# A fused conv-attention and expert kernel: the last image's row scatters pause in every fourth expert step

## The chip, the cores and the metric

One core of a Trainium2 chip (trn2). The metric is the device time of one execution in microseconds, the median of the runs. The profile is of one further execution; its span is longer than the runs' times.

## What is computed

Four images of 128 channels and 32 x 32 pixels pass through three kinds of attention (compressed, selected blocks, windows), a gated sum and a residual. That part fills the first 560 us and isn't touched. Its result t, 1024 tokens of 128 numbers per image, then goes through a mixture of experts, of which only this matters:

```python
logits = xt @ Wr + br                       # 8 experts
top_p, top_idx = top_k(softmax(logits), 2)  # two experts per token
xn = layernorm(xt)                          # no gain or bias yet
xe = xn * ln_g[e] + ln_b[e]
h = gelu(xe @ W1[e] + b1[e])                # 128 -> 512
y = h @ W2[e] + b2[e]                       # 512 -> 128
out = sum over the two chosen experts of weight * y
result = t + out
```

All is float32.

## The kernel before

Each engine has its own instruction stream, written out by hand, and semaphores between them. Tokens are not computed by every expert. Every token is copied twice, once for each expert that it picked, into an array in HBM, `xs_d`, which is sorted by expert. A row is 130 numbers: the 128 of the normalised token, its weight, and the row number where its result belongs. The copying is done by scatters: an indirect DMA issued by GpSimd (POOL) takes 128 rows from `pay` in SBUF and sends each to its place (`scatter_row`, L758). An image has 1024 tokens and two picks, so sixteen scatters (`2 * NT`, NT = 8). All scatters count up one semaphore, `scattered`.

The rows are then handled in tiles of 128, each of a single expert. The images form two batches (`BATCH`, images 0 and 1, images 2 and 3). Each batch has 39 tiles (`NTILE`), 78 in all (`NALL`); the second batch's first tile is number 39. An expert step k does these things, each by its engine:

- PE: the first matrix product for tile k - 3 (L2091), the transposes of tile k's rows (L2105), the second product for tile k - 5 (L2109).
- ACT: copies the expert's weights for tile k + 2 (L1052), gelu of tile k - 3 (L1067).
- DVE: adds the bias to tile k - 5 (L1574), applies gain and bias to tile k (L1579), multiplies tile k - 5 by the token weights (L1586).
- POOL: scatters the finished tile k - 5 to `z_d` in HBM with an indirect DMA (L780). In the text this is called the store of tile k - 5.
- SP: loads rows of tiles ahead of PE into a ring of 12 slots (`load_rows`, L619 and L620). Load n waits for the store of tile n - 12, which frees the slot. The queue is in order.

There are 83 steps (`NSTEP`). The first four run beside the last image's selected attention. The last image's router runs in steps 10 to 15 (`STEP_TT`, `STEP_RT`, `STEP_RK` = 15), so its picks are known only then. Its sixteen scatters are put into POOL's steps from 16 on, one in each, ahead of the step's store. POOL's queue is in order as well: a scatter goes out behind the store of the step before it.

SP asks for the scatters at one place. Before load 39 it runs `rows_written(1)`, which waits for all pad rows, for all 64 scatters of the four images, and for the second batch's table of tiles. Loads 40 and on are behind it in the queue. Between loads 28 and 36 SP also copies eight blocks of pad rows (`tail_pad`, L605). After load 50 it loads image 0's results back from `z_d` (`load_sums`, L632), which DVE adds up and PE transposes after step 49 (L1671).

Of the kernel before, what the change touches and what calls it, by code (L numbers as in the profile page):

```python
# [82 lines left out]
XROOM, WROOM, YROOM, HROOM = 8, 4, 8, 2  # L83
NSTEP = NALL + Y_LAG

SCATTER_OF = 100
PAD_AT = 28
ROWS_EARLY = 0
STEP_AT = 7
# [193 lines left out]
def build(nc, x, wqkv_c, wqkv_s, wqkv_w, w1k, w1v, w2k, w2v, gate_w1, gate_w2, projs, wr, fw1, fw2, fb1,  # L283
# [3 lines left out]
    with ExitStack() as ctx:  # L287
# [377 lines left out]
        def _(pool):  # L665
# [85 lines left out]
            def scatter_row(b, k, t):  # L751

                if t == 0:
                    pool.wait_ge(pay2_ready if k else pay_ready, b + 1)
                    if k:
                        pool.wait_ge(pay_ready, b + 1)
                    pool.nop(nofuse=True)
                gp.indirect_dma_start(xs_d, bass.IndirectOffsetOnAxis(pos[:, NT * k + t:NT * k + t + 1], 0),  # L758
                                      pay[:, k, t, :], None).then_inc(scattered, 16)
# [47 lines left out]
            for k in range(STEP_RK + 1, NSTEP):  # L807
                if sent < 2 * NT and k % SCATTER_OF != 0:
                    scatter_row(B - 1, sent // NT, sent % NT)
# [1427 lines left out]
```

## Time and profile before

| | us |
|---|---|
| median of 3 runs | 764.18 |
| lowest and highest run | 763.24 to 765.53 |
| span of the profiled execution | 791.0 |
| PE busy | 657.4 (83%) |
| VectorE (DVE) busy | 518.3 (66%) |
| ScalarE (ACT) busy | 427.1 (54%) |
| GpSimd (POOL) busy | 236.0 (30%) |
| scatters of rows by POOL (L758) | 64 of about 1 us |
| stores of tiles by POOL (L780) | 78 of about 1 us |

Times of the rows are microseconds from the start of the profiled span, which is 27 us longer than the median run. PE means the matmul stream, PEld the weight loads beside it, SPq the sequencer of SP. Some programs' names in a row stand for a ring: `xwin` and `wx_room` are both slots of expert weights, `xrow_room` and `qwT` of loaded rows, `xhatT` and `xblk` of finished tiles. Each float32 matmul shows as two records. A releaser in brackets is inferred; "issue" means that the profile shows nothing that the engine waited for.

### The profile page before, as it was taken

How to read it: one execution, taken by the hardware profiler on the slowest of the kernel's cores; microseconds unless marked ns; L12 is line 12 of the kernel's file. 1: busy time of each engine (PE TensorE's matmuls, PEld its weight loads, DVE VectorE, ACT ScalarE, POOL GpSimd, SP SyncE). 2: the span in 40 equal slices, each digit the busy share in tenths (PEclk: the TensorE clock that was granted, in tenths of full speed). 3: DMA queues.
4: the chain of work that ended last, by engine and by line, in shares of the span. 5: the costliest groups of instructions: out<-in, count | busy, mean ns of one | idle time of the engine just before them, and what ended most of it. 6: DMA issues, size and time to landing. Idle time of an engine off the chain costs nothing.

```text
span 791.0 us, 16898 instructions
## 1 busy us (share of the span) xinstructions
PE 657.4 (83%) x5198; PEld 497.5 (63%) x5198; DVE 518.3 (66%) x1757; ACT 427.1 (54%) x1259; POOL 236.0 (30%) x341
## 2 busy tenths in 40 slices
PE   2998999995999997889998687776879868979972
PEld 1684686663577655548664455543778757979971
DVE  4208678858977966887895678779766323554433
ACT  1228725555843563773355375335757545968851
POOL 3100142002024542004353200515243544533540
PEclk9999999997999999799999877857999979999995
DMA  8200000001000010000003700021014222253214
GB/s 304 105 0 28 2 6 1 2 1 54 0 3 5 25 32 27 1 0 5 2 28 94 202 1 1 8 49 52 21 32 132 59 65 72 72 185 89 66 44 163
DMA packets 36331, 40.27 MB, mean 51 GB/s; under 512 B 12164, under 2 KB 27796, under 8 KB 35956
## 3 DMA queue, kind: packets, MB, share of 16 engines
q1 hardware_dynamic: 30388, 27.70, 12.0%
q0 software_dynamic: 4704, 9.40, 3.6%
q10 hardware_dynamic: 1152, 2.10, 0.7%
q8 instruction: 44, 0.72, 0.4%
q14 instruction: 43, 0.35, 0.1%
HBM read 25.87 MB, written 15.17 MB: 52 GB/s over the span
## 4 chain that ended last, share of the span: by engine, by line
DVE 38%; PE 37%; issue 7%; another core or an unknown queue 5%; POOL 3%; DVEq 3%; ACT 3%; DMA 3%; SPq 1%; POOLq 0%; ACTq 0%
DVE nmx L1195 6%; PE ps L1731 6%; PE ps L1671 5%; PE ps L1676 4%; DVE r_P L1205 4%; DVE t_tok L1320 3%; DVE x_tok L1180 3%; PE ps L2091 3%; PE ps L2109 3%; PE ps L1815 3%; DVEq L1573 2%; PE ps L1746 2%; DVE xwin L1579 2%; PE ps L1788 2%
## 5 line engine op out<-in xcount | busy, mean ns | idle before, releaser
L906 ACT ACTIVATE r_P<-ps,nmx 128x225 f32<-128x225 f32 (+1 forms) x192 | 86.1, 470 | 67.3 <-DVE nmx L1195 65.6
L1574 DVE TENSOR_TENSOR hv<-ps,x_sb 128x128 f32<-128x128 f32 x78 | 22.7, 291 | 96.1 <-remote 50.1
L758 POOL DMA_INDIRECT xs_d<-pay,pos x64 | 66.7, 1042 | 61.4 <-DVE r_P L1205 38.6
L1195 DVE TENSOR_REDUCE nmx<-ps 128x4 f32<-128x900 f32 (+1 forms) x64 | 73.3, 1154 | 4.1 <-PE ps L1788 3.4
L780 POOL DMA_INDIRECT z_d<-xhatT,xrow_room x54 | 51.8, 959 | 78.5 <-DVE xhatT L1586 60.9
L1671 PE MATMUL ps<-ident,r_P 128*128 128x128 f32 (+1 forms) x384 | 59.0, 300 | 16.5 <-DVE R L1220 11.9
L1671 PEld LDWEIGHTS ps<-ident,r_P 128*128 128x128 f32 (+1 forms) x384 | 49.3, 162 | 36.0 <-DVE r_P L1205 22.8
L2091 PE MATMUL ps<-xwin,wx_room 128*128 128x128 f32 x416 | 61.2, 291 | 4.8 <-issue 4.2
L682 POOL TENSOR_TENSOR rstd<-vpe,minus_half 128x8 f32<-128x8 f32 x8 | 13.3, 1666 | 167.8 <-DVE vpe L1139 167.8
L2091 PEld LDWEIGHTS ps<-xwin,wx_room 128*128 128x128 f32 x416 | 55.2, 205 | 7.3 <-issue 6.0
L732 POOL TENSOR_TENSOR r_gh<-r_gh,nmw 113x392 f32<-113x392 f32 (+1 forms) x20 | 15.5, 774 | 148.3 <-DVE nmw L1234 148.0
L1746 PE MATMUL ps<-r_vc,w_sb 128*128 128x225 f32 x256 | 58.8, 375 | 0.0
L1746 PEld LDWEIGHTS ps<-r_vc,w_sb 128*128 128x128 f32 x256 | 46.1, 188 | 19.4 <-issue 15.9
L1731 PE MATMUL ps<-r_kc,w_sb 128*128 128x225 f32 x256 | 58.3, 375 | 0.0
L1788 PE MATMUL ps<-kbd,qT 64*128 64x450 f32 x128 | 39.7, 636 | 20.4 <-ACT r_P L906 20.4
L1205 DVE TENSOR_SCALAR r_P<-r_P,rZ 128x225 f32<-128x225 f32 (+1 forms) x192 | 54.1, 345 | 1.7
L1731 PEld LDWEIGHTS ps<-r_kc,w_sb 128*128 128x128 f32 x256 | 46.3, 188 | 6.6 <-issue 0.4
L2109 PE MATMUL ps<-w_sb,r_vc 128*128 x320 | 45.6, 286 | 5.2 <-issue 4.6
L2109 PEld LDWEIGHTS ps<-w_sb,r_vc 128*128 128x128 f32 x320 | 41.3, 200 | 6.4 <-issue 6.2
L1788 PE MATMUL ps<-kbd,qTs 64*128 64x512 f32 x128 | 43.9, 705 | 1.0 <-ACT r_P L906 1.0
L2109 PE MATMUL ps<-w_sb,qT 128*128 x304 | 42.1, 282 | 0.4 <-ACT qT L1067 0.2
L906 ACT ACTIVATION_READ_ACCUMULATOR r_P<-ps,nmx 128x1 f32 x192 | 41.1, 214 | 0.0
(233 smaller groups left out, 1488.4 us busy)
## 6 DMA issues: line engine op xcount, KB each, us to landing
xrow_room<-xs_d SPq DMA_DIRECT2D x54, 65.0 KB
x_sb<-x SPq DMA_DIRECT2D x4, 512.0 KB, 3.6
w_sb<-w1k SPq DMA_DIRECT2D x1, 2048.0 KB, 8.6
w_sb<-w1v SPq DMA_DIRECT2D x1, 2048.0 KB, 13.0
w_sb<-fw SPq DMA_DIRECT2D x1, 2048.0 KB, 9.3
w_sb<-fw SPq DMA_DIRECT2D x4, 512.0 KB, 9.7
r_vw<-z_d SPq DMA_DIRECT2D x8, 256.0 KB
kbdw<-z_d SPq DMA_DIRECT2D x8, 256.0 KB, 5.1
```

The source lines that it names most:

```text
L758: gp.indirect_dma_start(xs_d, bass.IndirectOffsetOnAxis(pos[:, NT * k + t:NT * k + t + 1], 0), pay[:, k, t, :], None).then_inc(scattered, 16)
L780: gp.indirect_dma_start(z_d, bass.IndirectOffsetOnAxis(xrow(n)[:, C + 1:C + 2].bitcast(U32), 0), yrow(n), None).then_inc(y_out[n % XRING], 16)
L906: last = sc.activation(Pb[t % NRING][:, h, 0:m], bank(name)[:, (h % 2) * m:(h % 2) * m + m], ACT.Exp, bias=nmx[:, t % NRING, h:h + 1], acc ...
L1195: ve.tensor_reduce(nmx[:, t % NRING, :].rearrange("p (a h) -> p a h", a=2), v.rearrange("p a (h m) -> p a h m", h=2), AX.X, ALU.max, negat ...
L1205: last = ve.tensor_scalar(v, v, rZ[:, t % NRING, h:h + 1], None, ALU.mult)
L1671: last = tr(bank(name)[0:m, k * j:k * j + k], src, ident[0:k, 0:k])
L1676: mm(bank(name)[:, 0:n], weights, rhs, start=True, stop=True).then_inc(full_sem(name), 1)
L1731: last = mm(bank(f"mk@{h}")[:, NB * a:NB * a + NB], w1k_sb[:, s, C * a:C * a + C], kcT[:, r:r + 2 * NBH - 1:2, c:c + 2 * NBH - 1:2], start ...
L1746: last = mm(bank(f"mv@{h}")[:, NB * a:NB * a + NB], w1v_sb[:, s, C * a:C * a + C], vcT[:, r:r + 2 * NBH - 1:2, c:c + 2 * NBH - 1:2], start ...
L1788: mm(bank(name)[:, 0:2 * m], q[p0:p0 + 64, 128 * t:128 * t + 128], kbd[p0:p0 + 64, :, 0:m], start=True, stop=True).then_inc(full_sem(name), 1)
L2091: last = mm(bank(f"fh{k}")[:, C * c:C * c + C], wx(n)[:, C * c:C * c + C], xe[:, n % 4, :], start=True, stop=True)
L2109: last = mm(bank(name)[:, 0:C], hT(n)[:, 128 * c:128 * c + 128], fw_sb[:, bass.ds(e, 1), W1X + C * c:W1X + C * c + C].rearrange("p a n -> ...
```

## The change

One constant. In the loop that writes POOL's steps, a scatter is put into step k only when k is no multiple of `SCATTER_OF`. With 100 this leaves out nothing between steps 16 and 31. With 4 it leaves out steps 16, 20, 24, 28, 32 and 36, so that the sixteenth scatter is in step 37.

```diff
-SCATTER_OF = 100
+SCATTER_OF = 4
```

The loop that reads it:

```python
sent = 0
for k in range(STEP_RK + 1, NSTEP):
    if sent < 2 * NT and k % SCATTER_OF != 0:
        scatter_row(B - 1, sent // NT, sent % NT)
        sent += 1
    expert_step(k)
```

## Rows read from the trace of the kernel before

**Rows 1.** The page's first line.
```profile
span 791.0 us, 16898 instructions
```

**Rows 2.** Timeline of PE: transposes of steps 39 and 43 (start, duration, line).
```profile
676.18 0.27 PE L2105 MATMUL ps<-ident,xrow_room 128*128 128x128 f32 x1
...
683.76 0.27 PE L2105 MATMUL ps<-ident,xrow_room 128*128 128x128 f32 x1
```

**Rows 3.** Busy time in windows: PE, PEld, DVE, ACT, POOL, clock, DMA share, GB/s.
```profile
620.00:640.00 20.00, 14.10 (x90) 13.52 (x91) 5.33 (x19) 10.75 (x32) 9.87 (x11) 0.85 0.20 58
...
720.00:740.00 20.00, 19.62 (x173) 19.16 (x172) 8.12 (x27) 17.38 (x52) 9.06 (x10) 1.00 0.23 65
```

**Rows 4.** The chain that ended last, 618 to 730 us (start, length, what).
```profile
618.83 4.16 another core or an unknown queue
...
629.70 7.23 another core or an unknown queue
...
642.04 2.59 another core or an unknown queue
...
646.43 4.93 another core or an unknown queue
...
656.53 6.07 another core or an unknown queue
...
727.39 2.21 another core or an unknown queue
```

**Rows 5.** Timeline of PE inside the second of these pieces.
```profile
635.39 0.27 PE L2091 MATMUL ps<-xwin 128*128 128x128 f32 x1 [1.05 <-issue]
```

**Rows 6.** Timeline of POOL, 609 to 689 us.
```profile
609.34 0.96 POOL L758 DMA_INDIRECT xs_d<-pay,pos  x1 [0.30 <-issue]
...
620.99 0.96 POOL L758 DMA_INDIRECT xs_d<-pay,pos  x1 [0.30 <-issue]
...
634.34 0.96 POOL L758 DMA_INDIRECT xs_d<-pay,pos  x1 [0.30 <-issue]
639.44 0.96 POOL L780 DMA_INDIRECT z_d<-xhatT,xrow_room  x1 [4.14 <-DVE xhatT L1586]
...
653.89 0.96 POOL L780 DMA_INDIRECT z_d<-xblk,qwT  x1 [4.47 <-DVE xblk L1586]
...
660.20 0.95 POOL L758 DMA_INDIRECT xs_d<-pay,pos  x1 [0.30 <-issue]
665.11 0.95 POOL L780 DMA_INDIRECT z_d<-xhatT,xrow_room  x1 [3.95 <-DVE xhatT L1586]
...
673.69 0.95 POOL L780 DMA_INDIRECT z_d<-xhatT,xrow_room  x1 [3.19 <-DVE xhatT L1586]
675.16 0.95 POOL L780 DMA_INDIRECT z_d<-xhatT,xrow_room  x1 [0.52 <-issue]
...
688.04 0.95 POOL L780 DMA_INDIRECT z_d<-xhatT,xrow_room  x1 [1.32 <-DVE xhatT L1586]
```

**Rows 7.** The chain again, 688 to 698 us: store of tile 38, SP, the sums.
```profile
688.04 2.40 DMA z_d<-xhatT,xrow_room
...
690.46 0.28 SPq L619
...
691.18 0.34 SPq L620
...
693.01 5.01 DMA r_vw<-z_d
```

**Rows 8.** Timeline of SP: loads 5 to 8, and load 39.
```profile
529.67 3.65 SPq L620 DMA_DIRECT2D xrow_room<-xs_d  x4
...
672.23 0.34 SPq L620 DMA_DIRECT2D xrow_room<-xs_d  x1
```

**Rows 9.** The page's DMA issues: KB each, median us from issue to landing.
```profile
r_P<-xblk SPq DMA_DIRECT2D x32, 8.0 KB, 1.7
...
out<-x_tok ACTq DMA_DIRECT2D x8, 256.0 KB, 2.1
```

## The prediction, made before the change was built

> **What bounds the kernel now.** I read the windows first, then the chain that ended last, then the timelines of POOL, PE and SP. The whole span is 791.0 us [rows 1]; the change touches only the last quarter, where 78 tiles of 128 routed rows go through the experts in 83 steps. Undisturbed, a step costs PE 1.895 us: the row transposes of steps 39 and 43 start at 676.18 and 683.76, four steps in 7.58 us [rows 2]. In 720 to 740 us PE is busy 19.62 of 20 us; in 620 to 640 us, where the scatters in question go out, only 14.10 of 20 [rows 3]. So PE sets the pace except where it is held up, and the question is what holds it up beside the scatters.
>
> The chain gives the gaps. Between 618 and 663 us it has five long pieces put down to "another core or an unknown queue", 4.16, 7.23, 2.59, 4.93 and 6.07 us, 25.0 us in all; later such a piece is about 2.2 us [rows 4]. There is no other core: in these pieces PE's matmuls come one by one, about 1.05 us of idle time before each, with no engine named as releaser [rows 5]. POOL's timeline shows what goes with it. POOL sends two indirect DMAs per step, a scatter of the last image (xs_d<-pay) and the store of a finished tile (z_d<-...), each 0.96 us long and 1.26 us apart when queued. The last before a gap's end stops at 621.95, 635.30 and 661.15 us (start plus length), and the gaps in the chain end at 622.99, 636.93 and 662.60: 1.0, 1.6 and 1.5 us later [rows 4, 6]. I take it as a pattern, not an explanation: PE runs about four steps, then crawls until POOL has emptied its queue. A cycle of four steps with four scatters is 14.45 us (store at 639.44 to store at 653.89), one without any 8.58 us (665.11 to 673.69) [rows 6].
>
> **The change, part by part.** The edit changes the order of POOL's queue alone. Now the sixteen scatters stand in steps 16 to 31. After it, steps 16, 20, 24, 28, 32 and 36 carry none, so they stand in 17-19, 21-23, 25-27, 29-31, 33-35 and 37. Three things follow.
>
> Taken out of the held-up stretch. The scatter of step 16 starts at 609.34 [rows 6], before the first long gap; moving it gains nothing. Those of steps 20, 24 and 28 stand last in POOL's queue while PE is waiting (the ones of 20 and 24 start at 620.99 and 634.34 [rows 6]). Without each, POOL is empty one slot earlier: 1.26 us, or (14.45 - 8.58) / 4 = 1.47 us by the difference of the cycles. Gain 3.8 to 4.4 us, and zero if POOL isn't what PE waits for.
>
> Put into the later stretch. Steps 33 to 35 get three scatters. The cycle that begins with the store at 665.11 takes 8.58 us now. With them POOL has four stores and three scatters: 1.47 us to the second store (as 673.69 to 675.16), six slots of 1.26 us, 1.4 us from the last op's end to the restart (the mean of the three above), and 2.5 us from restart to the next store (636.93 to 639.44) [rows 4, 6], 12.9 us in all. Cost 4.3 us, and zero by the same reason. The two parts cancel to within 0.5 us: I take 0, with -4.4 and +4.3 as ends.
>
> Moved past a wait. This part decides. SP loads the rows of the tiles from xs_d in order. Before row 39, the first of the second batch, it waits for all 64 scatters. Now the last scatter starts at 660.20 [rows 6]; with the 2.40 us that the store of 688.04 takes to land [rows 7] it is in by 662.6, and SP issues load 39 only at 672.23 [rows 8], for PE's use at 676.18 [rows 2]. The wait is free by 9.6 us. After the change the last scatter is that of step 37, queued on POOL behind the store of tile 31, which step 36 makes. What follows is serial:
> - from the transposes of a step to the store that it makes: 683.76 to 688.04, 4.28 us [rows 2, 6]
> - the scatter's slot behind it: 1.26 us
> - from its start to its landing: 2.40 us [rows 7]
> - SP from there to its issue: 690.44 to 691.18, 0.74 us [rows 7]
> - the load of 65 KB to landing has no row; a load of 8 KB takes 1.7 us and a store of 256 KB 2.1 us [rows 9]. I take 1.9, between these ends.
>
> Sum 10.6 us after the transposes of step 36. PE wants the row three steps later, at 3 x 1.895 = 5.7 us, and so waits 4.9 us. By clock times of the profile, with the store of tile 31 at 675.16 [rows 6]: 675.16 + 1.26 + 2.40 + 0.74 + 1.9 = 681.46, against 676.18, is 5.3 us. I take 5.1. It is shorter only where PE is late at step 39 for another reason, and longer by up to 3 us where POOL is behind at step 36.
>
> The Trainium skill ("DMA: Bandwidth & Descriptors", Anatomy of one DMA) states for a DMA issued by GpSimd a fixed 2.0 us plus the bytes over 436e3. An estimate by it for the 65 KB load is 2.15 us; the wait would be 5.3 to 5.6 us. No row here shows this load to landing.
>
> Who waits behind it: SP's loads 40 to 50 queue behind load 39. Unhindered SP issues four in 3.65 us [rows 8], 1.1 us each, faster than PE's 1.9, so only the first is late. Next is the load of image 0's sums, which needs the store of tile 38 and then 5.01 us of DMA [rows 7]; PE waits for it after step 49 already. Tile 38 is made in step 43, behind the new wait, so that stall moves along and doesn't swallow the 5.1 us. Nothing else before the end reads the scatters' semaphore.
>
> **Sum.** 0 + 5.1 = +5.1 us on a profiled span of 791.0. The runs have a median of 764.18, 27 us under the profiled span; the long gaps may be partly an effect of profiling. The new wait is made of DMA latencies and a queue, and I carry it over unchanged: 764.2 + 5.1 = 769.3 us.
>
> **The rivals.**
> (a) Without the profiler the gaps don't exist, and PE never stops among the scatters. POOL then has no rest from 620.99 on. Now, with a scatter in that slot, 23 slots of 1.26 lead to the store of tile 26 at 650.0; with 2.40 + 0.74 + 1.9 its ring slot gives row 38 at 655.0. PE, at 620.99 - 4.28 = 616.7 with step 20, wants it 18 steps later at 650.8, so it waits 4.2 us today. After the change 29 slots lead to the last scatter at 657.5 and to row 39 at 662.6, wanted at 652.7: 9.9 us. The difference is 5.7 us: 769.9. The 27 us speak for it, the coupling of gap and POOL against. It ends where the forecast does, and I count them together.
> The Trainium skill ("Runtime: NRT & Kernel Launch", Instruction fetch mechanics) says that crossing a block of instructions is mostly hidden; by that rule the gaps aren't code loading, or are none without the profiler, which is (a). The trace doesn't settle it: it shows crawling matmuls without a cause [rows 5].
> (b) Faster: the gap is caused by the very scatter that POOL issues while PE is held. The pauses of 20, 24 and 28 fall on those. If each cycle's gap sinks to the short 2.2 us, that is 25.0 - 4 x 2.2 = 16.2 us, less 5.1: 753. Halved, 761. For it: pauses and gaps share a period of four steps. Against: three scatters and four stores stay in each cycle, and the gap's end follows the last op by 1.0 to 1.6 us wherever it stands. It decides from the point where a pause saves over 1.7 us (5.1 / 3).
> (c) No difference: PE reaches step 39 late anyway, since the scatters of 33 to 35 lengthen the gap at step 37, or the pauses save their upper bound and the added ones cost little. 764 to 766.5.
> (d) Much slower: POOL is behind at step 36 by 3 us, and SP, hindered beside POOL's DMAs, stays late for the sums. 773 to 777.
> (e) That the edit does nothing is excluded: by 100 no step from 16 to 31 is divided, by 4 steps 16, 20, 24 and 28 are.
>
> **How the numbers follow.** Forecast with (a): 0.57 (767 to 773). (b): 0.12. (c): 0.20. (d): 0.11. The range 762 to 774 takes in the forecast, (c) and the near edges of (b) and (d), 8 in 10. About 0.3%, 2.3 us, is what a measurement of this kernel can tell from no change. Slower by more: 0.68; within: 0.20; faster: 0.12.
>
> **What would show it.** In the profile of the changed kernel: the last xs_d<-pay stands between the stores of tiles 31 and 32; SP's wait ahead of load 39 is put down to the scatter; the transposes of step 39 come about 7 us after those of step 38, where it is 1.9 now; the gaps at 622, 636 and 651 us end 1.3 us earlier each, and the one at step 37 grows. The forecast is wrong if step 39 comes without a pause, or if the cycles of four steps with scatters shrink to 10 us.

## The result, and the profile after

The change makes the kernel slower: 771.34 us against 764.32 us, medians of four runs each, a ratio of 1.0092 (95% interval 1.0070 to 1.0114), so +7.0 us with an interval of +5.3 to +8.7 us. The forecast was +5.1 us, 769.3.

The spans, though, are 791.0 us [rows 1] and 768.2 us, the wrong way round. One look at a kernel can mislead, and this one did. The kernel before was therefore profiled once more in the first experiment; that span is 763.2 us. All comparisons below use this second look unless they name the first, and the section on the reasons says what it does to the prediction.

The page of the changed kernel, with PE's row of slices and the clock:

```profile
span 768.2 us, 16898 instructions
...
PE 646.4 (84%) x5198; PEld 490.5 (64%) x5198; DVE 518.7 (68%) x1757; ACT 429.7 (56%) x1259; POOL 236.6 (31%) x341
...
PE   2999999995989999598998948778698998799992
...
PEclk9999999997999999799999969856999999999995
```

The windows of the changed kernel, which answer to [rows 3] (length, then busy time of PE, PEld, DVE, ACT and POOL with instruction counts, granted clock as a share of full speed, DMA share, GB/s):

```profile
620.00:640.00 20.00, 18.65 (x162) 18.11 (x161) 8.86 (x28) 16.72 (x48) 15.13 (x16) 1.00 0.38 98
640.00:660.00 20.00, 12.84 (x105) 11.93 (x104) 6.27 (x21) 12.64 (x36) 14.41 (x15) 0.99 0.33 85
...
720.00:740.00 20.00, 20.00 (x182) 20.00 (x181) 9.16 (x32) 17.45 (x53) 9.79 (x11) 1.00 0.26 68
```

In 620 to 640 us PE is busy 18.65 us where the first look at before had 14.10: the long gaps of [rows 4] are gone. The loss is in 640 to 660. Its place shows in PE's timeline of the changed kernel, the row transposes of steps 20, 38, 39, 40 and 41, which answer to [rows 2]:

```profile
612.89 0.27 PE L2105 MATMUL ps<-ident,qwT 128*128 128x128 f32 x1
...
652.88 0.27 PE L2105 MATMUL ps<-ident,xrow_room 128*128 128x128 f32 x1
660.34 0.45 PE L2105 MATMUL ps<-ident,xrow_room 128*128 128x128 f32 x1 [5.40 <-DMA xrow_room<-xs_d]
663.62 0.27 PE L2105 MATMUL ps<-ident,xrow_room 128*128 128x128 f32 x1
665.51 0.27 PE L2105 MATMUL ps<-ident,xrow_room 128*128 128x128 f32 x1
```

and steps 20, 38, 39 and 40 in the second look at the kernel before:

```profile
613.45 0.27 PE L2105 MATMUL ps<-ident,qwT 128*128 128x128 f32 x1
...
655.24 0.30 PE L2105 MATMUL ps<-ident,xrow_room 128*128 128x128 f32 x1 [0.31 <-DMA xrow_room<-xs_d]
657.26 0.27 PE L2105 MATMUL ps<-ident,xrow_room 128*128 128x128 f32 x1
659.16 0.27 PE L2105 MATMUL ps<-ident,xrow_room 128*128 128x128 f32 x1
```

Read as differences, they split the loss. From step 20 to 38 the changed kernel needs 39.99 us, before 41.79: a gain of 1.80. From 38 to 39 it needs 7.46 against 2.02: a loss of 5.44, of which 5.40 stand in the row as idle time ended by the load of the rows. From 39 to 40 it needs 3.28 against 1.90: a loss of 1.38. In all 50.73 against 45.71 us, +5.02. The spans differ by 5.0 as well, because what lies around this stretch cancels: up to step 20 the changed kernel is 0.6 us earlier, and from step 40 to the end it takes 104.6 us against 104.0. The medians differ by 7.0; where the other 2 us come from is told at the end.

The chain that ended last, in the changed kernel, goes through the links that the prediction named (start, length, what); it answers to [rows 7]:

```profile
655.21 2.30 DMA xs_d<-pay,pos
657.51 0.02 SPq L618
...
657.57 0.27 SPq L619
...
658.29 1.91 DMA xrow_room<-xs_d
...
660.34 0.45 PE ps L2105
```

The last scatter starts at 655.21 and lands at 657.51, SP issues load 39 at 658.29, it lands at 660.20, and PE goes on at 660.34. SP's list of waits has 7.6 us for the time that SP stood at the scatters' semaphore:

```profile
SPq L618 <- DMA xs_d<-pay,pos: 7.6, 1, 7.6
```

### The profile page after: what moved, and what is told of

It is laid out like the page before. It is cut to its first block, busy times and chain, and to the rows that moved or that the text cites. A ratio compares the mean times of both kernels' runs of the same rounds, so it can differ in the third digit from the quotient of the medians.

```text
span 768.2 us, 16898 instructions
## 1 busy us (share of the span) xinstructions
PE 646.4 (84%) x5198; PEld 490.5 (64%) x5198; DVE 518.7 (68%) x1757; ACT 429.7 (56%) x1259; POOL 236.6 (31%) x341
## 4 chain that ended last, share of the span: by engine, by line
PE 45%; DVE 35%; issue 6%; DMA 4%; POOL 4%; ACT 3%; SPq 2%; DVEq 1%; POOLq 0%; ACTq 0%
DVE nmx L1195 6%; PE ps L2091 6%; PE ps L1731 6%; PE ps L2109 6%; PE ps L1671 5%; DVE r_P L1205 4%; PE ps L1676 4%; DVE t_tok L1320 4%; PE ps L1815 3%; DVE x_tok L1180 3%; PE ps L1746 2%; PE ps L1845 2%; PE ps L1788 2%; DVE r_gh L1205 2%; ACT r_P L906 2%
## 5 line engine op out<-in xcount | busy, mean ns | idle before, releaser
L1671 PE MATMUL ps<-ident,r_P 128*128 128x128 f32 (+1 forms) x384 | 56.5, 291 | 15.1 <-DVE R L1220 10.7
L1671 PEld LDWEIGHTS ps<-ident,r_P 128*128 128x128 f32 (+1 forms) x384 | 47.0, 156 | 34.1 <-DVE r_P L1205 23.2
L2091 PE MATMUL ps<-xwin,wx_room 128*128 128x128 f32 x416 | 58.1, 285 | 0.0
L2091 PEld LDWEIGHTS ps<-xwin,wx_room 128*128 128x128 f32 x416 | 53.4, 201 | 0.7 <-issue 0.4
L1731 PEld LDWEIGHTS ps<-r_kc,w_sb 128*128 128x128 f32 x256 | 46.4, 188 | 6.6 <-issue 0.4
L2109 PE MATMUL ps<-w_sb,r_vc 128*128 x320 | 43.0, 278 | 0.0
L2109 PEld LDWEIGHTS ps<-w_sb,r_vc 128*128 128x128 f32 x320 | 39.3, 194 | 0.5 <-issue 0.4
```

Source lines behind the costliest of these rows:

```text
L1671: last = tr(bank(name)[0:m, k * j:k * j + k], src, ident[0:k, 0:k])
L1731: last = mm(bank(f"mk@{h}")[:, NB * a:NB * a + NB], w1k_sb[:, s, C * a:C * a + C], kcT[:, r:r + 2 * NBH - 1:2, c:c + 2 * NBH - 1:2], start ...
L2091: last = mm(bank(f"fh{k}")[:, C * c:C * c + C], wx(n)[:, C * c:C * c + C], xe[:, n % 4, :], start=True, stop=True)
L2109: last = mm(bank(name)[:, 0:C], hT(n)[:, 128 * c:128 * c + 128], fw_sb[:, bass.ds(e, 1), W1X + C * c:W1X + C * c + C].rearrange("p a n -> ...
```

## The experiments

Two theories were set against each other. W: the loss comes from the place of the last scatter alone, through the wait ahead of load 39. P: it comes from the pauses, which spread POOL's work over more steps. The table gives for each kernel the distance in us from the transposes of step 20 to those of steps 38, 39 and 40, read from PE's timeline as above, and the ratio to before. The distances come from one traced execution of each kernel, the ratios from all its runs.

| kernel | last scatter in step | 20 to 38 | 20 to 39 | 20 to 40 | ratio (95% interval) |
|---|---|---|---|---|---|
| before, second look | 31 | 41.79 | 43.81 | 45.71 | |
| pauses, last in 31 | 31 | 41.76 | 43.65 | 45.55 | 1.0019 (0.9996 to 1.0042) |
| pads early | 31 | 41.76 | 43.65 | 45.55 | 0.9985 (0.9966 to 1.0004) |
| every eighth | 34 | 40.04 | 43.55 | 45.56 | 1.0017 (1.0000 to 1.0035) |
| every eighth, pads early | 34 | 40.85 | 43.66 | 45.68 | 1.0006 (0.9984 to 1.0029) |
| one late, in 35 | 35 | 40.79 | 44.33 | 46.36 | 1.0019 (1.0005 to 1.0034) |
| pauses, last in 35 | 35 | 39.37 | 43.52 | 47.09 | 1.0025 (1.0006 to 1.0045) |
| one late, in 37 | 37 | 40.24 | 47.14 | 50.84 | 1.0083 (1.0050 to 1.0115) |
| the change | 37 | 39.99 | 47.45 | 50.73 | 1.0092 (1.0070 to 1.0114) |
| every third | 38 | 38.71 | 49.17 | 52.88 | 1.0097 (1.0061 to 1.0132) |
| the change, sixteen transposes added | 37 | 38.73 | 47.36 | 50.67 | 1.0060 (1.0040 to 1.0081) |
| the change, forty-four added | 37 | 39.00 | 48.18 | 50.17 | 1.0062 (1.0042 to 1.0082) |

**The kernel before once more.** No edit.

> The kernel before, profiled once more, to have a second look at it: the changed kernel's span was 768.2 us with none of the long gaps, the first profile of before 791.0 us with them. If the gaps belong to the profiled execution and not to the kernel, the span is now 760 to 765 us, the transposes of steps 20 to 28 are 1.9 us apart, and the first late row is one of 36 to 38. If they belong to the order of POOL's queue, the five long pieces come back and the span is about 790.

Measured: a span of 763.2 us, a run of 765.0 us. The transposes of steps 21 to 28 are 1.9 us apart, the first late row is that of step 30, where 36 to 38 was expected, and no piece of the chain between 590 and 690 us is put down to an unknown queue. So the five long pieces of [rows 4] belong to that one profiled execution, not to the order of POOL's queue. None of the eleven other profiles taken for this case, of kernels with nearly the same queue, has them either. What made them is not known.

This look shows what really bounds the stretch. POOL has no rest: from 613 us on, until the last scatter has gone out, its queue is full, store and scatter in turn, the last scatter at 647.16:

```profile
642.10 0.96 POOL L758 DMA_INDIRECT xs_d<-pay,pos  x1 [0.30 <-issue]
643.37 0.96 POOL L780 DMA_INDIRECT z_d<-xhatT,xrow_room  x1 [0.30 <-issue]
644.63 0.96 POOL L758 DMA_INDIRECT xs_d<-pay,pos  x1 [0.30 <-issue]
645.90 0.96 POOL L780 DMA_INDIRECT z_d<-xhatT,xrow_room  x1 [0.30 <-issue]
647.16 0.96 POOL L758 DMA_INDIRECT xs_d<-pay,pos  x1 [0.30 <-issue]
```

A step costs POOL 2.53 us here and PE 1.9. The stores free the ring slots, so from step 30 on PE gets its rows late, in before too: steps 20 to 38 take 41.8 us where 18 x 1.895 = 34.1 would do. SP issues load 39 at 654.41:

```profile
654.41 0.34 SPq L620 DMA_DIRECT2D xrow_room<-xs_d  x1
```

With the 2.30 us that the changed kernel's last scatter took, this kernel's is in by 649.5, which is 4.9 us before load 39 goes out; SP needs 0.8 us of that, and 4.2 are room. Counted from step 20, the change moves the start of the last scatter from 33.7 to 42.3 us. That is 8.6 us, 4.4 more than the room, and load 39 does go out 4.4 us later, at 45.4 and not at 41.0.

**One scatter late, no pauses.**

```diff
-    if sent < 2 * NT and k % SCATTER_OF != 0:
+    for _ in range(int(k < 31 or k == 37) if sent < 2 * NT else 0):
```

> No pauses: fifteen scatters in steps 16 to 30, the sixteenth held back to step 37. Theory W (the wait for the last scatter ahead of load 39 makes the loss): the whole loss is back, +5 to +8 us, 769 to 772. Theory P (the pauses spread POOL's work and slow the stores, or the rows, between steps 16 and 37): no loss beyond 1 us, since only one scatter has moved.

Measured: 771.05 us against 765.13, ratio 1.0083 (1.0050 to 1.0115). A single moved scatter brings the whole loss; 20 to 40 takes 50.84 us, the change's 50.73. W holds, and P falls, since there are no pauses here.

**The pauses, with the last scatter where it was.**

```diff
-    if sent < 2 * NT and k % SCATTER_OF != 0:
+    for _ in range({17: 2, 18: 2, 19: 2, 20: 0, 24: 0, 28: 0}.get(k, 1) if sent < 2 * NT else 0):
```

> The pauses of steps 20, 24 and 28 as in the change, but the last scatter stays in step 31: steps 17 to 19 carry two each. Theory W: no loss, 764 within 1.5 us. Theory P: half of the loss or more, 767 to 771.

Measured: 766.37 us against 765.13, ratio 1.0019 (0.9996 to 1.0042), and 45.55 us from 20 to 40, 0.2 less than before. The interval alone would allow up to 3.2 us; by the trace the pauses cost nothing. With sixteen scatters up to step 31, as before, they gain nothing either: step 38 comes after 41.76 us.

**Every third step.**

```diff
-SCATTER_OF = 100
+SCATTER_OF = 3
```

> A pause in every third step; the last scatter is in step 38, one step later than in the change. Theory W: the wait grows by the slot of the store of tile 32, 1.3 to 1.9 us over the change, so +8.3 to +8.9 us over before, 772.6 to 773.2. Theory P: the spreading is wider by one step in 22, no visible step over the change, 771.

Measured: 773.0 us against 765.13, ratio 1.0097 (1.0061 to 1.0132). From 20 to 40 it takes 52.88 us, 2.15 more than the change; the timeline has the idle time at step 39 as 8.33 us:

```profile
664.01 0.45 PE L2105 MATMUL ps<-ident,xrow_room 128*128 128x128 f32 x1 [8.33 <-DMA xrow_room<-xs_d]
```

W expected 1.3 to 1.9 us more than the change for the wait. Step 39 comes 1.72 us later (49.17 against 47.45), as expected; the other 0.43 us is the clock after the wait, treated below. The runs can't separate this kernel from the change.

**Every eighth step.**

```diff
-SCATTER_OF = 100
+SCATTER_OF = 8
```

> Pauses in steps 16, 24 and 32; the last scatter is in step 34. Theory W (the time follows the place of the last scatter): POOL works without rest from about 608 us, so this scatter starts near 651.4, as the fifteenth one of the change did; landed at 653.7, row 39 is there at 656.4, 43.6 us after the transposes of step 20, where before needs 43.8. No loss: 764 within 1.5 us. Theory P (the pauses themselves cost): half of the pauses, half of the loss, +2.5 to +3.5 us.

Measured: 767.05 us against 764.79, ratio 1.0017 (1.0000 to 1.0035). The interval reaches from 0 to 2.7 us, so the runs alone exclude neither W's zero nor the lower edge of P's 2.5 to 3.5. The trace does: 45.56 us from 20 to 40, before 45.71. Step 39's distance is 43.55 where 43.6 was worked out. Its row does not come in time:

```profile
659.04 0.30 PE L2105 MATMUL ps<-ident,xrow_room 128*128 128x128 f32 x1 [1.45 <-DMA xrow_room<-xs_d]
```

SP waits 3.5 us for the last scatter and PE 1.45 us for the row, but step 38 came 1.75 us earlier than before, and the two cancel.

**One scatter late, in step 35, and the change with step 16 not paused.**

```diff
-    if sent < 2 * NT and k % SCATTER_OF != 0:
+    for _ in range(int(k < 31 or k == 35) if sent < 2 * NT else 0):
```

> Fifteen scatters in steps 16 to 30 and the last in step 35, two steps earlier than in the run with one late scatter. Theory W with POOL's queue full: it starts two slots of 1.26 us earlier, near 652.6, and row 39 is ready 44.4 us after step 20's transposes against 43.8: +0.6 us and no fall of the clock, 764.5 to 766. If instead the wait grew by a whole step of PE for each step of delay and began at step 31, +3 to +4 us.

```diff
-    if sent < 2 * NT and k % SCATTER_OF != 0:
+    for _ in range(int(k % 4 != 0 or k == 16) if sent < 2 * NT else 0):
```

> The change with step 16 not paused: pauses in 20, 24, 28 and 32, the last scatter in step 35. Theory W: it starts near 652.7, row 39 is ready 44.9 us after step 20's transposes: +1.1 us, 765 to 767. Theory P: four of the six pauses are there, +4 to +5 us, 768 to 769.

Measured: 765.83 and 766.30 us against 764.79, ratios 1.0019 (1.0005 to 1.0034) and 1.0025 (1.0006 to 1.0045). The first has step 39 at 44.33 against the 44.4 expected, and its clock does not fall: +0.65 us from 20 to 40. The second has step 39 at 43.52, 1.4 earlier than expected and 0.3 earlier than before. Its last scatter started at 651.88 and not at 652.7, and its step 20 came 0.6 us later than in the change. Yet from 20 to 40 it needs 47.09 us, 1.4 more than before, because step 40 follows 39 after 3.57 us, at a granted clock of 0.63 (the column before the last two):

```profile
657.00 0.45 PE L2105 MATMUL ps<-ident,xrow_room 128*128 128x128 f32 x1 [2.09 <-DMA xrow_room<-xs_d]
660.57 0.27 PE L2105 MATMUL ps<-ident,xrow_room 128*128 128x128 f32 x1
...
656.00:660.00 4.00, 3.00 (x14) 3.03 (x15) 0.03 (x1) 0.73 (x2) 1.60 (x2) 0.63 0.41 115
```

So at step 35 the wait begins to be felt, and in the second kernel what is felt is the clock after it and not the wait. By step 37 it is +5.

**SP's pad copies earlier, alone and with every eighth step.**

```diff
-PAD_AT = 28
+PAD_AT = 20
```

> The kernel before with SP's eight pad copies after loads 20 to 27 instead of 28 to 35. The second look at before shows the loads of rows 32 to 36 issued about 1.7 us after their slot is free, because a pad copy is in the way. If SP is what makes rows 30 to 38 late, the time falls by up to 1.7 us, 762.5 to 764. If POOL's pace of 2.52 us per step is, which holds back the stores that free the slots, it stays within 0.5 us.

> A version that might beat both: pauses in steps 16, 24 and 32 with the last scatter in step 34, and SP's pad copies after loads 20 to 27. The pauses alone brought step 38 forward by 1.75 us and lost it to the wait; early pads alone brought nothing at step 38. If the wait ahead of load 39 sets the time, this one is where before is, 764 to 766. If SP's queue was what took the gain, it is 1 to 2 us faster, 763.

Measured: 763.62 against 764.79 us, ratio 0.9985 (0.9966 to 1.0004), and together 765.90 against 765.48, ratio 1.0006 (0.9984 to 1.0029). Neither is told from before by its runs. From 20 to 38 the early pads alone take 41.76 us, as before, so by the trace SP's copies are not what makes the rows late.

**PE kept busy while it waits.** In the changed kernel step 40 follows 39 after 3.28 us. The windows give a reason, the column before the last two being the granted clock:

```profile
656.00:660.00 4.00, 0.00 (x0) 0.00 (x0) 0.00 (x0) 0.75 (x2) 2.08 (x3) 0.97 0.23 66
660.00:664.00 4.00, 3.66 (x21) 3.69 (x22) 0.61 (x2) 0.18 (x1) 0.00 (x0) 0.61 0.26 58
664.00:668.00 4.00, 4.00 (x38) 4.00 (x38) 1.81 (x6) 3.75 (x12) 1.35 (x2) 1.00 0.26 64
```

After standing idle PE gets 0.61 of its clock in the mean, 21 matmuls in four microseconds where the next four have 38: most of that stretch is at 1.2 GHz, the lower of the two levels. The Trainium skill ("TensorE: Matmul & The Clock Gate", What's actually happening) states that the clock is gated between 1.2 and 2.4 GHz by how busy PE has been. The trace agrees: the mean of 0.61 comes after PE's idle time and lies between the two levels.

```diff
+    if k == NTILE[0]:
+        for _ in range(16):
+            tr(bank(name)[:, C:2 * C], ident[:, :], ident[:, :])
     if k < NALL:
         pe.wait_ge(*row_loaded(k))
```

The second kernel has 44 in place of 16. PE makes these transposes in step 39, ahead of its wait for row 39; nothing uses them.

> The changed kernel, with sixteen transposes of the identity added on PE in step 39 ahead of its wait for row 39; their bank is overwritten by the row's own transpose. At about 0.22 us each they fill 3.6 us of the 5.4 us in which PE stood idle there. In the changed kernel the granted clock of 660 to 664 us is 0.61 and step 39 to 40 takes 3.28 us against 1.90. If that is the price of PE's idling, step 40 now follows 39 after 1.9 us and the run is 1.4 us faster than the change, 5.0 - 1.4 = 3.6 us over before, 768.4. If the 3.28 us come from ACT and DVE standing empty, or from row 40 being late as well, they stay and the time is that of the change, +5 to +7 us.

> As the run with sixteen added transposes, with forty-four. The sixteen took 1.91 us together (0.12 us each, not 0.22), PE still stood idle for 4.83 us, the granted clock fell to 0.73 in 660 to 664 us, and step 40 came 3.3 us after step 39. Forty-four fill about 5 us and leave 1 to 2 us idle. If idling is what costs the 1.4 us, the clock stays at 1.0 and step 40 follows after 1.9 us; the distance from step 20 to step 40 falls from 50.7 to about 49.3 us. If ACT and DVE or row 40 are the cause, it stays 3.3 us. A median of runs can just tell 1.4 us: 769 to 770 against 771.

Measured: with sixteen, 1.0060 (1.0040 to 1.0081). One took 0.12 us and not 0.22, so PE still stood idle for 4.83 us; the granted clock fell to 0.73 in 660 to 664 us, and step 40 followed after 3.31 us. This run leaves the question open. With forty-four the timeline is

```profile
650.14 4.97 PE L2105 MATMUL ps<-ident 128*128 128x128 f32 x44
657.43 0.33 PE L2108 MATMUL ps<-ident,xrow_room 128*128 128x128 f32 x1 [2.32 <-DMA xrow_room<-xs_d]
...
659.42 0.27 PE L2108 MATMUL ps<-ident,xrow_room 128*128 128x128 f32 x1
```

and the clock of 656 to 660 and 660 to 664 is

```profile
656.00:660.00 4.00, 2.57 (x23) 2.57 (x24) 0.54 (x2) 0.37 (x2) 0.00 (x0) 1.00 0.28 73
660.00:664.00 4.00, 4.00 (x39) 4.00 (x38) 1.94 (x7) 3.76 (x12) 1.53 (x2) 1.00 0.32 82
```

The clock stays at full, at 2.4 GHz, and step 40 follows after 1.99 us instead of 3.28. ACT and DVE stood just as empty, so they are not the cause: by these traces some 1.3 us are the price of the clock. The distance from step 20 hides it (50.17 us against 50.73), since in this look step 20 itself came early. From the start of the last scatter, 652.31 here and 655.21 in the change, step 40 comes after 7.11 us against 8.41.

Two reservations. The traced run is the fastest of its eleven, 766.08 us where their median is 770.29, and the ratio of all, 1.0062 (1.0042 to 1.0082), isn't told from that of the change, nor from that with sixteen. And the length of a wait does not alone say whether the clock falls. It fell after the four longest, 4.77 to 8.33 us; of the waits near 2 us it fell after 2.09 (the second kernel with its last scatter in step 35) and 1.92 (every eighth with early pads, 0.69 in 652 to 656 us), and not after 1.85 (before), 2.26 (early pads) and 2.32. What decides between those is not shown.

## Why the prediction came out as it did

**Moved past a wait: right, link by link.** This step carried the forecast. It gave 2.40 us to landing, 0.74 for SP, 1.9 for the load and 5.1 for PE's wait; measured were 2.30, 0.78 (657.51 to 658.29), 1.91 and 5.4. The experiments show it as cause: one scatter alone in step 37 brings the loss, and from step 34 on the distance from 20 to 40 grows with the step of the last scatter, 45.6, 46.4 to 47.1, 50.7 to 50.8 and 52.9 us. The ratios part only 37 and 38 from the rest. Of the signs that the prediction named, the first three came: the last scatter stands between the stores of tiles 31 and 32, SP's wait is put down to it, and step 39 comes 7.46 us after 38. The fourth, gaps that end earlier, did not, since there are none. The bounds on the load's landing (1.7 and 2.1) held. The estimate by the Trainium skill ("DMA: Bandwidth & Descriptors", Anatomy of one DMA), 2.15 us by its sum for a DMA issued by GpSimd, was 0.24 too long; this load is issued by SP. One term was mis-sized: from step 36's transposes to the last scatter it had 4.28 + 1.26 = 5.5 us, and it took 6.9 (648.34 to 655.21), because POOL was behind by 1.3 us. The prediction had this as a condition, up to 3 us. The wait was still only 0.3 us over the forecast, since step 38 came 0.75 us late as well and PE wanted row 39 later. The margin before the change, 9.6 us in the prediction, was 4.9 in the second look.

**Taken out and put in: zero by luck.** Both parts rested on the gaps of [rows 4, 6], and the pattern that PE waits for POOL's queue to empty. Neither the changed kernel nor before's second look has those gaps. The step that failed is the reading "cycle with scatters 14.45, without 8.58", and with it the price of 1.26 to 1.47 us per pause. Even the first look didn't bear the pattern out in full: it was drawn from three of the five pieces, and the third piece ends at 644.63, where POOL has a store at 644.49 and a scatter at 645.75 and no rest. What the pauses did goes through the ring: with fewer scatters ahead of a store, its slot is free sooner, and step 38 came 1.80 us earlier. The run with three of the pauses and the last scatter in step 31 shows that they do this only by moving scatters behind step 31, not by their place. The gain is not in proportion to the scatters moved: one brings 1.0 and 1.55 us in its two kernels, the change's four bring 1.80. What limits it was not looked into. The prediction set zero for the sum with ends of 4.4 on both sides, so the 1.8 lay inside.

**Not foreseen: the clock.** The wait costs 5.4 us and then 1.4 more, as PE comes back at the lower clock. In the kernels with one late scatter in 37 and with every third step it is 1.8 (step 40 after 3.70 and 3.71 us). The forecast carried a wait of over 5 us and did not ask what PE's clock does after it. The first profile had the sign of it: 0.86 as the mean clock of 600 to 660 us, with the gaps in it, against 0.97 in the second look. By the traces -1.8 + 5.4 + 1.4 is +5.0: the missing gain and the missing term nearly cancel, and so the forecast's nearness of 0.1 us to the traces is in part luck. A forecast with the clock and without the gain would have been +6.5.

**What is left.** The traces give +5.0, the medians +7.0. The traced execution of the change is the fastest of its four runs, 770.0 us against the median of 771.34, and that of before, 765.0, is 0.7 above the median of before's four. These two make up the 2.0 us, so nothing beyond the spread of the runs asks for an explanation. In the experiments the kernel before ran 88 times more, with a median of 765.2; against that the change is +6.2. The spread goes with the clock: in every kernel the runs with a lower mean granted clock tend to be the slower ones. Over whole runs that mean is 0.929 in before, and 0.925, 0.925 and 0.924 in the change, with one scatter late in 37 and with every third step. That fits a price of the clock after long waits, without proving it.

**The rivals.** The prediction counted (a) together with the forecast, and (a) was the route that was taken: PE has none of the gaps among the scatters, POOL has no rest, the ring makes rows late, and the last scatter comes late. Its numbers were off: it had 4.2 us lost to late rows in before, where 41.79 - 34.1 = 7.7 were, and 9.9 after the change, where it is 47.45 - 19 x 1.895 = 11.4. Their difference, 5.7, is above the 3.6 by which step 39 came later, because before loses more to late rows than it had reckoned; the clock then adds 1.4. One term of it is the store's landing, taken as 2.40 us, where the store at 648.43 took 3.88. Its argument from the Trainium skill ("Runtime: NRT & Kernel Launch", Instruction fetch mechanics), that crossing a block of instructions is mostly hidden, agrees with twelve profiles without such gaps; none of them shows what the gaps of the first were. (b) is dead: it needed the gaps. (c) missed, as PE was late by only 0.75 us between steps 36 and 38 for another reason. (d) had SP stay late for the sums; SP issued the loads after 39 every 1.11 us as predicted, and steps 41 to 49 run at 1.9 us.

## What to carry over

When a change moves the last of a set of transfers, look for whoever waits for all of them, and write its chain from that transfer to the engine that sets the pace, with the engine's own queue ahead of it. It is free until the chain is longer than the lead, and then it sets the pace: in the nine kernels with the last scatter in step 34 or later, PE reaches step 39 between 5.02 and 5.29 us after that scatter starts, where the prediction had 2.40 + 0.74 + 1.9 = 5.04. Counted to step 40, steps 31 to 34 cost nothing here, 35 about one microsecond, 37 five.

An idle time of several microseconds on PE can have a second price, the clock after it: 1.4 to 1.8 us here after waits of 4.8 us and more. And gaps with no releaser in one profiled execution that is 27 us longer than the runs are no base for a price: take a second look first.

## What the runs showed of the hardware

Some stores by POOL's indirect DMA land late while its queue is full. From the start of the instruction to landing, the stores on the chains after 665 us, where POOL has rests, take 2.05 to 2.40 us in all kernels [rows 7]. In the full stretch, from 613 to 650 us, those on the chains take anything from 2.26 to 4.02: 2.26 and 3.88 in before's second look, 3.28 in the changed kernel. The chain picks out the late ones, and whether the full queue or the other transfers of that stretch make them late is not shown:

```profile
648.43 3.88 DMA z_d<-xhatT,xrow_room
```

The time to landing therefore isn't a constant to be carried from a quiet stretch into a busy one. The last scatters, at the end of the full queue, landed after 2.29 to 2.44 us in nine kernels. POOL's own pace in the full queue is 0.96 us plus 0.30 us from one such instruction to the next, in the changed kernel as in before's second look.
